# A decoder layer over 16 batches: the loop on the engines written out

## The reference

```
x = x + self_attention(layernorm(x))       # one head, rotary tables, causal mask
x = x + cross_attention(layernorm(x), ctx) # 16 heads of 64, ctx: 1444 keys of 96 features
x = x + ffn(layernorm(x))                  # input rounded to 8 bits, ternary 128x128 weight, bias
```

## Time and profile before

| | us |
|---|---|
| runs | 1173.03, 1173.48, 1172.94 |
| median | 1173.03 |
| profiled execution | 1173.88 |
| its span, first to last instruction | 1170.9 |
| mean granted TensorE clock | 0.989 of full |

### The profile page before, as it was taken

The page is one execution under the profiler, slowest core; times in us unless marked ns, Lnnn a source line. Parts: engine busy times, 40 slices in busy tenths (PEclk is TensorE's granted clock), DMA queues, the critical chain, the costliest instruction groups (busy, mean ns, idle before and its releaser), DMA issues.

```text
span 1170.9 us, 20390 instructions
## 1 busy us (share of the span) xinstructions
PE 1136.2 (97%) x6561; PEld 1047.5 (89%) x6561; DVE 934.5 (80%) x1691; ACT 695.5 (59%) x1001; POOL 232.1 (20%) x228
## 2 busy tenths in 40 slices
PE   6799999999999999999999999999999999999996
PEld 5588999998999899998999989999899999999995
DVE  3698888887888788787978878898788888878645
ACT  1155656656575665756657565665656566575653
POOL 3120130312203022130302213030221303112010
PEclk9799999999999999999999999999999999999998
DMA  7101010010101001010010101001010100100000
GB/s 151 41 1 42 2 41 4 1 42 5 41 3 41 4 2 40 4 41 5 9 36 1 41 5 41 3 2 42 3 41 3 41 3 2 42 2 1 3 1 4
DMA packets 12727, 24.40 MB, mean 21 GB/s; under 512 B 4934, under 2 KB 8654, under 8 KB 12494
## 3 DMA queue, kind: packets, MB, share of 16 engines
q1 hardware_dynamic: 12622, 23.00, 7.4%
HBM read 21.88 MB, written 0.82 MB: 19 GB/s over the span
## 4 chain that ended last, share of the span: by engine, by line
PE 91%; DVE 5%; issue 3%; ACT 1%; DMA 1%; POOL 0%; DVEq 0%; SPq 0%; POOLq 0%; ACTq 0%
PE banks L1086 35%; PE banks L1116 31%; PE banks L940 10%; PE banks L978 4%; PE banks L931 4%; PE banks L960 1%; DVE pr_lo L887 1%; PE banks L1021 1%; DVE maxes L666 1%; PE banks L1011 1%; PE banks L1049 0%; DMA q_hi<-negmaxT 0%; DVE maxes L674 0%; DVE xn L650 0%; ACT banks L617 0%
## 5 line engine op out<-in xcount | busy, mean ns | idle before, releaser
L615 ACT ACTIVATE pr_hi<-banks 128x800 fp32r<-128x800 f32 x384 | 322.4, 840 | 393.4 <-PE banks L1086 393.4
L666 DVE TENSOR_REDUCE maxes<-banks 128x1 f32<-128x482 f32 x585 | 370.4, 653 | 57.6 <-PE banks L940 53.8
L887 DVE TENSOR_TENSOR pr_lo<-banks,pr_hi 128x800 fp32r<-128x800 f32 x320 | 315.0, 985 | 56.8 <-ACT banks L617 56.4
L617 ACT ACTIVATE banks<-banks 128x800 f32<-128x800 f32 x384 | 319.8, 833 | 0.0
L940 PE MATMUL banks<-cT_hi,q_hi 96*128 96x482 f32 x585 | 223.6, 382 | 1.4 <-DVE maxes L666 1.4
L1086 PE MATMUL banks<-q_hi,cT_hi 97*128 97x400 f32 x768 | 216.7, 363 | 8.3 <-DMA q_hi<-negmaxT 7.4
L1116 PE MATMUL banks<-pr_hi,cN_hi 128*97 128x400 f32 x768 | 214.2, 346 | 0.1
L1086 PE MATMUL banks<-q_hi,cT_lo 96*128 96x400 f32 x768 | 208.5, 352 | 0.0
L1086 PE MATMUL banks<-q_lo,cT_hi 96*128 96x400 f32 x768 | 204.4, 347 | 0.0
L1116 PE MATMUL banks<-pr_hi,cN_lo 128*96 128x400 f32 x704 | 190.6, 344 | 0.0
L1116 PE MATMUL banks<-pr_lo,cN_hi 128*97 128x400 f32 x704 | 190.6, 344 | 0.0
(11 more groups left out here) (116 smaller groups left out, 887.6 us busy)
## 6 DMA issues: line engine op xcount, KB each, us to landing
cT_raw<-in_ctxT SPq DMA_DIRECT2D x16, 568.5 KB
cN_raw<-in_ctx SPq DMA_DIRECT2D x16, 528.0 KB
out<-result SPq DMA_DIRECT2D x16, 50.0 KB
X<-in_x SPq DMA_DIRECT2D x1, 700.0 KB
cN_raw<-in_ctx_last SPq DMA_DIRECT2D x16, 40.5 KB
wqT<-in_wqT SPq DMA_DIRECT2D x1, 512.0 KB, 5.4
wo<-in_wo SPq DMA_DIRECT2D x1, 512.0 KB, 13.2
wkT<-in_wkT SPq DMA_DIRECT2D x1, 384.0 KB, 7.2
```

The costliest lines, as they stand in the source:

```text
L615: nc.scalar.activation(pr_hi[:, s % RING, :].rearrange("p (a q) -> p a q", a=2), pair, ACT.Exp, scale=float(DH) ** -0.5).then_inc(hi_done, 1)
L617: nc.scalar.activation(pair, pair, ACT.Exp, scale=float(DH) ** -0.5).then_inc(exp_done, 1)
L666: nc.vector.tensor_reduce(maxes[:, t, p:p + 1], here[:, 0:PW], AX.X, ALU.max).then_inc(misc_free, 1)
L887: nc.vector.tensor_tensor(pr_lo[:, s % RING, :].rearrange("p (a q) -> p a q", a=2), banks[:, slot:slot + 2, 0:BLK], pr_hi[:, s % RING, :]. ...
```

## The change

The loop is gone: all 16 batches are written out, one after another, on each engine. The batch number is a Python integer everywhere, so every wait has a constant, every address is fixed, and no register instruction stands between others. The class `Order`, which counts the links of a chain of operations on one engine, loses the part that served the loop.

```
-    LOOPED = B - 4
@@
-        def batches(eng, body):
-
-            body(0, 0)
-            with eng.Fori(0, LOOPED // 2) as i:
-                for h in (0, 1):
-                    body(i * 2 + (1 + h), 1 - h)
-            for b in range(LOOPED + 1, B):
+        def batches(body):
+
+            for b in range(B):
                 body(b, b % 2)
@@
             def enter(self, b):
-                if isinstance(b, int):
-                    if b == LOOPED + 1:
-                        self.count += LOOPED * self.each
-                    else:
-                        self.count += self.at
-                    self.base = self.count
-                else:
...
+                self.count += self.at
+                self.base = self.count
                 self.at = 0
@@
             def body(b, par):
-                ahead = b + 2 if isinstance(b, int) else sp.snap(b + 2)
-                before = b - 1 if isinstance(b, int) else sp.snap(b - 1)
...
-                    load_ctx(ahead)
+                    load_ctx(b + 2)
                 if present(b, -1):
-                    store(before, 1 - par, use_of(b, "F"))
+                    store(b - 1, 1 - par, use_of(b, "F"))
```

More of the change, by code:

```diff
@@ L267, in present @@
             if away == 0:
-                return isinstance(b, int) and b == (0 if what in BATCH_0 else B - 1)
-            return not isinstance(b, int) or 0 <= b + away < B
+                return b == (0 if what in BATCH_0 else B - 1)
+            return 0 <= b + away < B
         def length(b):
             return sum(present(b, away, what) for items in AT.values() for what, _, away in items)
-        FULLBODY = sum(away != 0 for items in AT.values() for _, _, away in items)
-        assert FULLBODY % FILLS == 0
         def base(b):
-            if isinstance(b, int):
-                return NSTART + sum(length(i) for i in range(b))
-            return NSTART + length(0) - FULLBODY + b * FULLBODY
+            return NSTART + sum(length(i) for i in range(b))
         def ring_bank(use):
@@ L289, in body_uses @@
             k, found = 0, []
-            parity = base(b if isinstance(b, int) else 1)
+            parity = base(b)
             for items in AT.values():
@@ L321, in decoder_layer, with __init__ @@
         class Order:
-            def __init__(self, eng, s, each):
-                self.eng, self.s, self.each = eng, s, each
+            def __init__(self, eng, s):
+                self.eng, self.s = eng, s
                 self.count = 0
                 self.at = 0
-                self.looped = False
             def enter(self, b):
-                if isinstance(b, int):
-                    if b == LOOPED + 1:
-                        self.count += LOOPED * self.each
-                    else:
-                        self.count += self.at
-                    self.base = self.count
-                else:
[L339 to L344, removed]
+                self.count += self.at
+                self.base = self.count
                 self.at = 0
@@ L428, in body @@
                     split_done(b + 1)
-                    load_ctx(ahead)
+                    load_ctx(b + 2)
                 if present(b, -1):
-                    store(before, 1 - par, use_of(b, "F"))
+                    store(b - 1, 1 - par, use_of(b, "F"))
                 if present(b, 1):
                     move_negmax(b + 1, 1 - par, use_of(b, "negmax"))
-            batches(sp, body)
+            batches(body)
             store(B - 1, 1, base(B) + TAIL.index(("F", 0)))
@@ L473, in padding @@
                 pool.wait_ge(const_s, made[0])
-            order = Order(pool, pchain, 4)
+            order = Order(pool, pchain)
             order.count = 2
@@ L547, in body @@
                     ffn_input(b - 1)
-            batches(pool, body)
+            batches(body)
             order.enter(B)
@@ L628, in body @@
                         self_exp(b + 2, par)
-            batches(act, body)
+            batches(body)
             evacuate(B - 1, 1, NB - 1)
@@ L635, in _ @@
         def _(dve):
-            order = Order(dve, vchain, 10)
+            order = Order(dve, vchain)
             order.base = 0
@@ L904, in body @@
                             consume(b + away, par if away % 2 == 0 else 1 - par, what, j, use, bank)
-            batches(dve, body)
+            batches(body)
             order.enter(B)
@@ L1137, in body @@
                             behind = [what] + behind[:FILLS - 2]
-            batches(pe, body)
+            batches(body)
             for s in range(STEPS - LAG, STEPS):
```

## The result

The median is 1164.05 us over six runs (1163.65 to 1164.64); the kernel before, on the same chips, 1172.70 (1172.02 to 1173.48, six runs). The ratio is 0.9927, 95% interval 0.9914 to 0.9939: 8.65 us faster. The profiled execution took 1164.64 us with a span of 1162.8.

What follows compares the result with a forecast made beforehand. PE was taken to set the pace everywhere, losing time only at the loop's five jumps back. 1173.03 us less 5 x 1.58 = 7.9, all other terms 0, gave 1165.1 us, range 1163.0 to 1168.3.

Steps and rivals of the forecast that it cites:

- The jumps: Five jumps back between batches: removing them saves 1.58 us each on PE, 7.9 us in all.
- What a jump costs, and where: At a looped batch border: 1.05 us visible PE gap, the rest of 1.58 slower steps while DVE catches up.
- Register arithmetic at nothing: Register instructions computing wait targets in the loop: hidden by PE's sequencer running ahead, 0 gain, at most 1.2 us.
- Entry, exit, order, buffers: Loop entry and fall-through taken as 0, at most 0.14 us; sequence of working instructions unchanged, nothing moved past a DMA.
- The lower clock at the end: TensorE clock of 0.50 from 1162.2 us on: moves with the end, taken as 0, about 1 us either way.
- The collision: Step 10: DVE's last-keys operation stands through two POOL operations; 0.58 us on PE, in one of 13 full batches, left at one.
- rival 1: Step 10: POOL comes earlier, more batches have DVE held up, 0.58 us each, all twelve 7.0; chance 0.06 beyond four extra.
- rival 2: Straight code starves engines of instructions beside context loads, 1.58 us per place, up to 1187 us; chance 0.05, 0.03 slower.
- rival 4: Longer program costs time outside the span, then 3.0 us; doubling it would give 1168.1 us; chance 0.03.

Runs made afterwards that it cites:

- e1: The looping kernel before, all engines still looping but in two passes of six batches, so one jump back instead of five: 1166.47 us.
- e2: The looping kernel before with only PE still looping (six passes of two batches), the other four engines in straight code: 1173.91 us.
- e3: The looping kernel before with only DVE still looping, the other engines in straight code: 1172.79 us.
- e11: The looping kernel before, all engines still looping but in three passes of four batches, so two jumps back: 1169.33 us.
- e12: The straight kernel of the result run again unchanged: 1163.69 us.
- e4: The looping kernel before with only ACT, POOL and SP still looping, PE and DVE in straight code: 1164.09 us.
- e9: The kernel of e2 run again unchanged, for a trace of a longer execution: 1171.42 us.

## Why the prediction was right

- *The jumps.* Forecast 5 x 1.58 = 7.9 us, measured 8.01 in the same stretches; e1 shows that jumps remain expensive when everything else of the loop stays. The step held.
- *What a jump costs, and where.* I split the 1.58 us into PE's own gap of 1.05 and DVE's catching up. The size was right, the picture of it not: by the starts of the matmuls PE's gap was 1.2 us, and e2 and e3 show that either stall alone costs almost the whole. The two stalls follow the same last step and run side by side, so a PE that is already 1.2 us late needs to wait little more for DVE (some 0.3 us behind this border, none in e2), and the sum was near the larger of the two. For a change that takes the jumps from all engines this makes no difference; for one engine alone my split would have promised 5 us and given about none.
- *Register arithmetic at nothing.* Shown by e1 and e11: plain stretches within the loop of 68.35 to 68.51 us, as without it.
- *Entry, exit, order, buffers.* Nothing of it shows in the trace after. The lower clock at the end begins later or earlier by a few us against the last work from trace to trace, with no effect that could be told.
- *The collision (rival 1).* Among the 13 full batches it stayed at one in the first trace and none in e12; rival 1 didn't come about. In the others DVE's operation ends 0.12 us behind POOL's multiplication, so it does get in between the two. But the price goes by how long DVE stands, not by whether it stands through both: 2.13 us in batch 13 of e4 cost PE 0.2, 2.48 us in batch 13 of e3 0.5, both behind the multiplication alone.
- *Straight code runs dry (rival 2).* PE is busy for the whole of 168 to 990 us, the waits of DVE put down to "issue" (five of 2.1 us before) are gone, and fewer instruction packets are moved.
- *Outside the span (rival 4).* I had feared growth, and there was none. Over 47 runs of the kernel before it lies between 1.75 and 3.13 us, median 2.0; over 23 runs of straight kernels and e4 between 1.76 and 1.85. The trace of before was a long case (3.0). In it a packet of queue q8 starts 1.9 us after the last instruction has ended, and in e9, with 2.0 us outside, one starts 1.0 us after; in the other twelve traces, with 1.75 to 1.85 us outside, q8 moves none there. That an execution lasts until such a packet is in would fit; two cases don't prove it.
- *The other 1.1 us.* The forecast was 1165.1, the result 1164.05. Of the difference 0.33 is the median of before, which came out lower with six runs than with three. The gain itself was 8.65 instead of 7.9: 0.1 more in the stretches, up to 0.1 in the rest of the span, 0.2 outside it (2.0 to 1.8 in the medians, not the 1.1 of the two profiled executions). The rest, some 0.35 us, is the choice of executions: the trace after is the longest of its six (span 1162.8, median 1162.25), while the trace of before is near the median of its spans (1170.9, 1170.7). None of this was in the forecast.

## What to carry to other kernels

Compare stretches of equal work between landmarks of the bounding engine; one written-out copy of a loop's body is the measure of what the loop costs. Hidden are the register instructions, not the jump back: 1.6 to 2.0 us here on a busy PE, whatever the body's length, so fewer and longer passes win part of it (one jump instead of five: 6.65 of 9 us; two: 3.6). Before taking a stall from one engine, ask which others stand at the same time: stalls side by side have to go together.

## What the runs showed that I had not expected

- A loop body of 189 rows on ACT goes back in 0.27 us without an instruction packet; one three times as long takes 2.5 us and moves one, like DVE's (2.1 us idle) and PE's (a branch of 3.3 to 3.9 us).
- A DVE stall of 2.1 us behind its jump reaches PE through what DVE does first after it, the rounding of the context for a small fill, not through the split of the numerators that PE's large matmuls wait for.
- With only PE looping, the executions spread over 6.5 us (1171.3 to 1177.8), those of the straight kernel over 1.1; the longer ones have the lower mean clock. Open.
